# Fetching 28 of the last tile's 128 label rows by the sync engine

## The reference

```
inputs         = front_emb[movie_id]                  # 2048 x 64, gathered
true_w, true_b = after_emb[labels], after_bias[labels]
samp_w, samp_b = after_emb[sampled_ids], after_bias[sampled_ids]
true_logits    = sum(inputs * true_w, -1) + true_b - log(expected_count(labels))
sampled_logits = inputs @ samp_w.T + samp_b - log(expected_count(sampled_ids))
sampled_logits = where(sampled_ids == labels, sampled_logits - 1e9, sampled_logits)
loss           = logsumexp([true_logits, sampled_logits]) - true_logits
```

## Time and profile before

| | us |
|---|---|
| median of 3 runs | 59.75 (59.63 to 59.86) |
| the profiled execution | 59.7 |
| its span, first to last instruction | 57.9 |
| POOL busy | 38.8 (67%) |
| DVE busy | 48.2 (83%) |
| ACT busy | 42.7 (74%) |
| PE busy | 33.8 (58%) |

### The profile page before, as it was taken

The page is one execution under the profiler, slowest core; times in us unless marked ns, Lnnn a source line. Parts: engine busy times, 40 slices in busy tenths (PEclk is TensorE's granted clock), DMA queues, the critical chain, the costliest instruction groups (busy, mean ns, idle before and its releaser), DMA issues.

```text
span 57.9 us, 608 instructions
## 1 busy us (share of the span) xinstructions
PE 33.8 (58%) x137; PEld 23.1 (40%) x137; DVE 48.2 (83%) x134; ACT 42.7 (74%) x70; POOL 38.8 (67%) x48
## 2 busy tenths in 40 slices
PE   0000083999939929996999699929918992000000
PEld 0000051826517708853777467707707770000000
DVE  2699888876879999999999958997999999995230
ACT  4303999688987759899998999489878789950020
POOL 4067677777667777767777767777766777776000
PEclk9999999999999999999999999999999999997555
DMA  0482222232010111100111001011011011110100
GB/s 0 161 198 63 46 46 46 66 68 54 23 23 23 31 35 24 23 23 23 23 43 26 23 23 40 23 36 33 23 23 23 23 32 36 24 23 23 23 0 6
DMA packets 1715, 2.17 MB, mean 38 GB/s; under 512 B 944, under 2 KB 944, under 8 KB 1712
## 3 DMA queue, kind: packets, MB, share of 16 engines
q0 software_dynamic: 1280, 1.59, 12.1%
q1 hardware_dynamic: 432, 0.55, 3.5%
HBM read 2.13 MB, written 0.01 MB: 37 GB/s over the span
## 4 chain that ended last, share of the span: by engine, by line
POOL 28%; DVE 26%; issue 14%; DMA 12%; ACT 9%; PE 5%; POOLq 2%; DVEq 0%
POOL w_rows L228 13%; POOL t_rows L228 13%; DVE psum L515 12%; DVE masks L407 9%; ACT psum L346 6%; DMA x_rows<-front,rows 4%; DMA t_rows<-after,rows 4%; DMA id_cols<-ids 3%; DVE xT L427 2%; POOLq L62 2%; ACT masks L328 2%; PE psum L297 2%; POOL x_rows L228 2%; PE psum L299 1%; PE psum L298 1%
## 5 line engine op out<-in xcount | busy, mean ns | idle before, releaser
L515 DVE CUSTOM_DVE_ANT_0 psum<-psum,masks 128x1024 f32<-128x1024 f32 x16 | 19.4, 1232 | 0.0
L346 ACT ACTIVATE psum<-psum,lowest 128x1024 f32<-128x1024 f32 x16 | 17.3, 1080 | 2.7 <-DVE lowest L515 2.7
L228 POOL DMA_INDIRECT x_rows<-front,rows x16 | 15.1, 945 | 4.9 <-issue 4.6
L228 POOL DMA_INDIRECT t_rows<-after,rows x16 | 15.1, 943 | 4.9 <-issue 4.3
L297 PE MATMUL psum<-wT_high,xT 128*128 128x512 f32 x32 | 13.5, 420 | 4.9 <-ACT psum L346 3.8
L299 PE MATMUL psum<-b_parts,ones 128*128 128x512 f32 x32 | 12.7, 396 | 0.0
L298 PE MATMUL psum<-wT_low,xT 128*128 128x512 f32 x32 | 12.6, 394 | 0.0
L228 POOL DMA_INDIRECT w_rows<-after_twice,rows x8 | 7.7, 967 | 4.0 <-issue 2.1
L407 DVE TENSOR_SCALAR_CACHE_REDUCE masks<-sample_f,label 128x1024 f32<-128x1024 f32 x8 | 10.2, 1277 | 0.2
L297 PEld LDWEIGHTS psum<-wT_high,xT 128*128 128x128 f32 x32 | 6.0, 187 | 8.6 <-issue 5.1
L328 ACT ACTIVATE masks<-sample_ids,neg_label 128x1024 f32<-128x1024 int32 x8 | 9.1, 1139 | 0.0
(11 more groups left out here) (80 smaller groups left out, 33.6 us busy)
## 6 DMA issues: line engine op xcount, KB each, us to landing
sample_ids<-sample_row SPq DMA_DIRECT2D x1, 512.0 KB, 4.1
x_rows<-front,rows POOLq DMA_INDIRECT x16, 2.4
t_rows<-after,rows POOLq DMA_INDIRECT x16, 2.4
w_rows<-after_twice,rows POOLq DMA_INDIRECT x8, 2.6
id_cols<-ids SPq DMA_DIRECT2D x1, 20.0 KB, 1.8
out<-loss SPq DMA_DIRECT2D x1, 8.0 KB, 1.4
```

The lines of the kernel that those rows point to most:

```text
L228: return pool.indirect_dma_start(dst, None, table, bass.IndirectOffsetOnAxis(ap=rows[:, col:col + 1], axis=0))
L346: nc.scalar.activation(logits(t), logits(t), ACT.Exp, bias=lowest[:, t:t + 1], scale=-1.0, accum_out=sums[:, t:t + 1]).then_inc(exp_ok, 1)
L515: V.tensor_tensor_reduce(out=logits(t), in0=logits(t), in1=masks[:, t, :], scale=1.0 / SHRINK, scalar=3e38, op0=ALU.add, op1=ALU.min, accu ...
```

## The change

The label row numbers of the last tile's last 28 examples (partitions 100 to 127) are made a second time, side by side in one partition. A third load at the start of SP's program brings their ids into `line_ids`, one row of 28. POOL makes a row of limits with a second iota. DVE does the clamping and wrapping on that row, three operations between the series and the count, and gives `line_rows`. SP waits for it and then, for each of the 28, loads a row number into a register (with a bounds test against the table's length) and issues a DMA of that one row of 65 values into its partition of `t_rows`. The last gather on POOL lists only 100 rows. The last `dot` waits for the gather and for all 28 single transfers. Nothing else of the program changes, and what is computed is the same.

```
+LINE = 28
+LINED = P - LINE

 # SP
             sp.dma_start(sample_ids[:, :], sample_row.rearrange("(a n) -> a n", a=1).to_broadcast([P, SAMPLES])
                          ).then_inc(row_in, 16)
+            sp.dma_start(line_ids[:, :], line).then_inc(line_in, 16)
+            sp.wait_ge(line_rows_ok, 1)
+            for p in range(LINE):
+                row = sp.value_load(line_rows[0:1, p:p + 1], min_val=0, max_val=VOCAB + SPREAD - 1)
+                sp.dma_start(t_rows[LINED + p:LINED + p + 1, TILES - 1, :], after[bass.ds(row, 1), :]
+                             ).then_inc(line_t_in, 16)
             sp.wait_ge(loss_ok, 1)

 # POOL
             pool.iota(limits[:, :], pattern=[[P, COLS]], base=VOCAB - 1, channel_multiplier=1).then_inc(limits_ok, 1)
+            pool.iota(line_limits[:, :], pattern=[[1, LINE]], base=VOCAB - 1, channel_multiplier=0
+                      ).then_inc(line_limits_ok, 1)
...
-                    gather(t_rows[:, t, :], after, LAB + t).then_inc(t_in[k], 16)
+                    if t < TILES - 1:
+                        gather(t_rows[:, t, :], after, LAB + t).then_inc(t_in[k], 16)
+                    else:
+                        pool.indirect_dma_start(t_rows[0:LINED, t, :], None, after,
+                                                bass.IndirectOffsetOnAxis(ap=rows[0:LINED, LAB + t:LAB + t + 1], axis=0)
+                                                ).then_inc(t_in[k], 16)

 # DVE
             for n in (4, 3, 2, 1, 0):
                 link(V.scalar_tensor_tensor(series[:, :], series[:, :], e[n], tries[:, :], ALU.add, ALU.mult))
+            dve.wait_ge(line_in, 16)
+            dve.wait_ge(line_limits_ok, 1)
+            V.tensor_scalar(line_wrap[:, :], line_ids[:, :], 0.0, float(VOCAB), ALU.is_lt, ALU.mult)
+            link(V.scalar_tensor_tensor(line_low[:, :], line_ids[:, :], float(-VOCAB), line_limits[:, :], ALU.max,
+                                        ALU.min))
+            V.tensor_tensor(line_rows[:, :], line_low[:, :], line_wrap[:, :], ALU.add).then_inc(line_rows_ok, 1)
...
                 dve.wait_ge(t_in[k], 16 * (b - a))
+                if b == TILES:
+                    dve.wait_ge(line_t_in, 16 * LINE)

 # the arrays given to the program
+        "line": got["r_target_movie_id"].reshape(P, TILES)[LINED:, -1].reshape(1, LINE),
```

More of the change, by code:

```diff
@@ L41, with log_uniform_loss @@
 LN2_LOW, LN2_HIGH = -0.00021219444, 0.6933594
-def log_uniform_loss(nc, ids, sample_row, front, after, after_twice, out):
+def log_uniform_loss(nc, ids, sample_row, line, front, after, after_twice, out):
     f32, f32r, i32 = mybir.dt.float32, mybir.dt.float32r, mybir.dt.int32
@@ L80, in log_uniform_loss @@
         sample_ids = sb("sample_ids", [P, SAMPLES], i32)
+        line_ids = sb("line_ids", [1, LINE], i32)
+        line_wrap = sb("line_wrap", [1, LINE])
+        line_limits = sb("line_limits", [1, LINE], i32)
+        line_low = sb("line_low", [1, LINE])
+        line_rows = sb("line_rows", [1, LINE], i32)
         ident = sb("ident", [P, P])
@@ L169, in log_uniform_loss @@
         labels_ok = sem("labels_ok")
+        line_in = sem("line_in")
+        line_limits_ok = sem("line_limits_ok")
+        line_rows_ok = sem("line_rows_ok")
+        line_t_in = sem("line_t_in")
         w_in = [sem(f"w_in{q}") for q in range(QUARTERS)]
```

## The result

| | before | after |
|---|---|---|
| median, 9 executions each | 59.69 us | 60.2 us |
| the profiled execution | 59.7 us | 60.36 us |
| its span | 57.9 us | 58.3 us |
| around the span, mean of the executions | 1.8 us (the profiled one) | 2.11 us |

The ratio is 1.0077, with a 95% interval of 1.0052 to 1.0102: 0.5 us slower. The time lies inside the predicted range and on the side that was not forecast.

The account below looks back on a forecast made before the run. POOL's unbroken run of forty gathers was taken to bound the kernel. From the 59.75 us median, -0.10 (gather) and +0.03 (wait), all else 0, gave -0.07 and 59.68 us; range 59.35 to 60.5 us.

Parts of the forecast that it names:

- The bound, and POOL running through: POOL runs through its forty gathers without waiting for scores; finishing the last one sets the kernel's end.
- Term 1: Last gather on POOL: 100 rows instead of 128 save 0.10 us, the middle between 0 (all fixed) and 0.21 (all per row).
- The rival of the dearer gather: Last gather on POOL takes 0.16 us more; kernel at 59.98 us, up to twice that extra; chance 0.10.
- the divisor rule: Transfer engines: the largest number up to 16 dividing the slowest dimension, 10 for 100 partitions; transfer 0.04 us longer.
- Term 2: Last gather's transfer, 1.50 us from POOL's end to landing: no change, 0 us; 0.04 saved or lost possible.
- Term 3: SP's 28 loads and transfers: hidden at a pitch of 1.13 us per row, cover gone from 1.49; cost 0.
- Term 4: Three added DVE operations push what follows by 0.53 us, absorbed by slack and tail idle time; cost 0.
- Term 5: SP's third load and POOL's iota cost 0; DVE's new wait before the last product costs 0.03 us.
- three signs that I had named for a wrong forecast: SP's transfer ends DVE's last idle time; a POOL gap exceeds 0.30 us; last landing over 1.50 us after POOL's end.
- the sign of being right: Last gather on POOL shorter than 0.94 us, with the same start near 52.3 us.

Follow-up runs that it names:

- short_gather: Kernel before with only the last gather cut to 100 rows, a constant in the 28 unfetched places, and one wait added on POOL; ratio 1.0070.
- iota_late: Kernel before with one unread 1x28 iota added on POOL behind the last gather; ratio 1.0063.
- iota_only: Kernel before with one unread 1x28 iota added on POOL, at the place where the change has it; ratio 1.0039.
- no_iota: Changed kernel without POOL's second iota; DVE clamps the 28 row numbers against a constant instead; ratio 1.0028 to the kernel before.
- after_again: The changed kernel run once more, unchanged, beside the kernel before on one chip; ratio 1.0109.
- list_beside: Changed kernel with all 128 rows in the last gather and SP's 28 rows sent to a spare tile nobody reads; ratio 1.0061 to the kernel before.
- line_of_32: Changed kernel without POOL's second iota, with 32 rows on SP and 96 in the last gather; ratio 1.0029 to the kernel before.
- front_only: Changed kernel without SP's 28 loads and transfers and DVE's wait for them, with 128 rows in the last gather; ratio 1.0086 to the kernel before.

## Why the prediction was wrong, point by point

**The bound, and POOL running through: right.** POOL's gaps stay at 0.30 to 0.31 us in the changed kernel, and in its two profiles the last product still comes 2.5 to 2.6 us after the last gather's start.

The sum said -0.07 us and the measurement +0.5. Two terms failed, the gather (-0.10, measured +0.06) and the iota (0, measured +0.27, around the span); the rest of the loss, 0.1 to 0.2 us in the span, has no proven cause.

**Term 1, the gather (-0.10): wrong in sign.** It costs 0.06 us more. The failing step is the choice of the middle between "all fixed" and "all per row". The earlier trace rows held a hint that I used for bytes only: the two groups of 16 gathers differ by 2 ns in the mean, and the gathers of `w_rows`, with twice the bytes, have a median of 946 ns (their mean of 967 holds the first, of 1.10 us). That points to a fixed price. The rival of the dearer gather had the mechanism right (a list that does not fall evenly costs POOL more) and its size too large (0.16). That the measured 60.2 us is also what this rival gives at twice its price is luck: of the 0.5 us, the last gather is 0.06. I gave the divisor rule a place at the transfer, where it was worth nothing that could be seen, and not at POOL's own time, where it was worth 0.06 us.

**Term 2, the transfer (0): right to 0.1 us**; from POOL's end to the landing short_gather shows 54.63 - 53.23 = 1.40 us against 1.50. The divisor rule holds in the packet counts, and the 0.04 us that it was to cost here can't be seen.

**Term 3, SP's list (0): right that it is hidden.** Its pitch was 1.27 us for 1.13 forecast, below the deciding 1.49. The Trainium skill's floor of 0.6 us for a load ("DMA: Bandwidth & Descriptors", Latency and other measured facts) is above the median of what the rows show for single numbers, 0.49 us, and inside their spread of 0.44 to 0.68: most loads were cheaper than that floor.

**Term 4, DVE (0): right.** The three operations took from 11.23 to 11.60 + 0.17 = 11.77 us, and the tail of DVE still waits for gathers, 0.37 us before tile 14 (0.64 before) and 0.98 before tile 15. DVE's timeline of the changed kernel:

```profile
11.23 0.17 DVE L516 TENSOR_SCALAR line_wrap<-line_ids 1x28 f32<-1x28 int32 x1
11.32 0.25 DVE L517 SCALAR_TENSOR_TENSOR line_low<-line_ids,line_limits 1x28 f32<-1x28 int32 x1
11.60 0.17 DVE L519 TENSOR_TENSOR line_rows<-line_low,line_wrap 1x28 int32<-1x28 f32 x1
```

**Term 5, the small rest (+0.03): wrong, and this is the half that was missed.** The new wait on DVE can't be seen: from POOL's end to the product are 1.59 us in the changed kernel and 1.64 before. What failed is the iota, counted at 0. I looked at what the iota hides under on POOL's timeline, found 1.8 us of idle time, and counted 0. That is true inside the span, as iota_late and iota_only show: their spans did not grow. But the sum had carried the 1.8 us around the span as a constant, and there the iota costs 0.27 us. Why one instruction more costs that is not known; that it does is shown by no_iota, iota_only and iota_late. No row of the kernel before could have given that number; what could be known is that the metric holds a part that the profile does not show, and that my sum had no bound for what an edit adds there.

None of the three signs that I had named for a wrong forecast came: SP's transfers did not end the last wait, the gaps on POOL stayed as before, and the landing took no longer than 1.50 us where it can be read (short_gather). All three look inside the span and past the gather's own length. Only the sign of being right, a last gather shorter than 0.94 us, failed.

**Inside the span**, four small terms recur in the profiles; three I did not have, and the gather I had with the other sign. SP's first issue takes 0.41 to 0.42 us in every kernel with the list and 0.38 in every one without, which moves everything behind it by 0.04. Its last one takes 0.38 to 0.39 us instead of 0.35 to 0.37, another 0.04. From the first gather's start to the second's it is 1.45 or 1.46 us in the kernels with a gather of 100 rows and 1.40 to 1.42 in those without: 0.05. And the last gather is the 0.06. Together 0.19 us, against a measured 0.24 to 0.31 us in the mean spans of no_iota and after_again. With the 0.27 around the span that makes 0.46 of the 0.5 us. The sum is counted from single profiles; list_beside agrees with it (0.08 counted, 0.05 measured) and line_of_32 as well, but front_only (0.2 measured, hardly 0.02 counted) and short_gather (-0.05 measured, 0.11 counted) do not. A standard error of 0.1 us allows such misses, but front_only's 0.2 us, without a list and without a short gather, is then as good a finding as no_iota's 0.24. So these terms are each seen in the profiles; that they make up the loss in the span is not shown, and the cause of that half stays open but for the 0.06 us of the gather.

## What to carry to other kernels

Before part of a batched instruction's list is moved elsewhere, ask for its fixed price: equal durations over different contents suggest that only whole instructions are worth removing, and a shorter list can cost more than the full one, as here every length did that 16 does not divide. A sum for an edit of a tenth of a microsecond needs the part of the metric that lies outside the profile as a term with bounds of its own; compare total less span between kernels before explaining anything inside. When a loss shows up, put each added instruction alone into the old kernel: here the least of them, an iota in idle time, was half of it.

## What was not expected of the hardware

- A gather's time on POOL against its rows: 0.89 us (32), 0.92 (64), 0.94 (80), 0.92 to 0.94 (96), 0.94 (112), 0.94 (128), but 1.00 to 1.06 (100), 0.99 (120) and 2.58 us (127).
- The time around the span goes up and down with the number of instructions in POOL's program, between 1.80 and 2.28 us. One more costs 0.27 us whether it stands ahead of the gathers or behind them.
- The first gather of a kernel with one of 100 rows costs 1.14 to 1.15 instead of 1.10 us (five kernels), though it is 49 us ahead of it; with one of 96 rows it costs 1.12 (line_of_32).
- SP's register load from SBUF takes 0.49 us for one number, but 1.4 and 3.1 us for 14.
- In two profiled executions (sems_only and iota_only) gather 38 took 1.44 and 1.41 us instead of 0.94, with nothing in the program to cause it: four unused semaphores in the one, an iota in idle time in the other, and neither kernel's mean span is longer by that much. That is half a microsecond in the span of one execution, and one reason why a single execution says little about a change of this size. POOL's timeline of iota_only:

```profile
48.39 0.94 POOL L231 DMA_INDIRECT t_rows<-after,rows  x1 [0.30 <-issue]
49.63 1.41 POOL L231 DMA_INDIRECT t_rows<-after,rows  x1 [0.30 <-issue]
51.34 0.94 POOL L231 DMA_INDIRECT t_rows<-after,rows  x1 [0.30 <-issue]
```
